# Moving the dense half and the coordinate products in TensorE's order of a fused attention and deformable-convolution kernel

## The reference, cut to what matters

```python
q, k, v = split(einsum('bchw,oc->bohw', group_norm(x), qkv_w) + qkv_b)   # 4 heads of 32
o = softmax(q @ k.T * hd**-0.5) @ v
feat_l = einsum(o, proj_w) + proj_b + x
...
offset_feat = conv1x1(concat([feat_l, feat_s * 2]), W_off)
om = conv3x3(offset_feat, W_om) + b_om            # 8 groups x 9 taps x (y, x, mask)
py, px = base + offset_y, base + offset_x         # per pixel, group and tap
val = bilinear(feat_s, py, px) * sigmoid(mask)    # four corners, zero outside
out = relu(einsum('bgckhw,ogck->bohw', val, W_dcn) + b_dcn) + feat_l
```

## Time and profile before

| what | value |
|---|---|
| median of 3 runs | 12684.2 us (12682.26 to 12689.32) |
| profiled execution, time | 12683.0 us |
| its span, first to last instruction | 12681.2 us |
| POOL busy | 10320.1 us (81%) |
| PE (TensorE matmul) busy | 9257.2 us (73%) |
| DVE (VectorE) busy | 7291.4 us (57%) |
| ACT (ScalarE) busy | 4747.5 us (37%) |
| POOL's indirect DMAs, L469 | 7168, mean 998 ns, with 949.5 us of issue between |
| POOL's additions, L465 | 13824, mean 250 ns |
| halves, L708, products | 12288, mean 356 ns |
| mean granted TensorE clock | 0.838 |

### The profile page before, as it was taken

The page is one execution under the profiler, slowest core; times in us unless marked ns, Lnnn a source line. Parts: engine busy times, 40 slices in busy tenths (PEclk is TensorE's granted clock), DMA queues, the critical chain, the costliest instruction groups (busy, mean ns, idle before and its releaser), DMA issues. The chain is left out here.

```text
span 12681.2 us, 168047 instructions
## 1 busy us (share of the span) xinstructions
PE 9257.2 (73%) x56052; PEld 5057.7 (40%) x56052; DVE 7291.4 (57%) x10291; ACT 4747.5 (37%) x6104; POOL 10320.1 (81%) x21509
## 2 busy tenths in 40 slices
PE   4677778775778777776577777777577777777754
PEld 1244444442444444443244344444234444444444
DVE  4356566644666666664566666665456666666443
ACT  1344444432434434433244344343233434334322
POOL 0278888885788888888488888888858888888888
PEclk7888888886888888888788888888788888888876
DMA  1222211110011111111011111111101111111100
GB/s 48 77 67 70 66 23 24 24 24 23 21 33 25 24 24 25 25 24 29 13 25 33 24 24 25 25 23 24 28 16 31 25 25 25 25 23 24 24 22 21
DMA packets 373774, 373.51 MB, mean 29 GB/s; under 512 B 129440, under 2 KB 219936, under 8 KB 372768
## 3 DMA queue, kind: packets, MB, share of 16 engines
q0 software_dynamic: 229376, 235.34, 8.9%
q10 hardware_dynamic: 97920, 71.35, 1.8%
q1 hardware_dynamic: 45472, 54.53, 1.6%
HBM read 316.66 MB, written 44.04 MB: 28 GB/s over the span
## 5 line engine op out<-in xcount | busy, mean ns | idle before, releaser
L469 POOL DMA_INDIRECT g<-patches,idx x7168 | 7156.6, 998 | 1112.4 <-issue 949.5
L905 DVE TENSOR_REDUCE mx<-ring 128x2 f32<-128x1024 f32 x2048 | 2411.1, 1220 | 2919.3 <-PE ring L666 2381.8
L541 ACT ACTIVATE p<-ring 128x1024 f32<-128x1024 f32 x2048 | 1984.8, 1021 | 3832.3 <-PE ring L724 2960.3
L465 POOL TENSOR_TENSOR carrier<-carrier 128x1 f32<-128x1 f32 x13824 | 3063.5, 250 | 122.0
L708 PE MATMUL ps_x<-fx,hats 128*128 128x208 f32 x12288 | 2520.1, 356 | 120.4 <-DVE hats L1048 78.8
L721 PE MATMUL ring<-qf,kf 32*128 32x512 f32 x8192 | 1459.9, 786 | 1515.3 <-ACT hats L551 816.3
L708 PEld LDWEIGHTS ps_x<-fx,hats 128*128 128x128 f32 x12288 | 2192.2, 196 | 671.2 <-issue 598.1
L734 PE MATMUL ps_a<-p,v 128*64 128x512 f32 x4096 | 1442.3, 790 | 39.0 <-DVE shared L932 37.6
L734 PE MATMUL ps_b<-p,v 128*64 128x512 f32 x4096 | 1247.2, 692 | 0.0
L1067 DVE TENSOR_TENSOR ps_x<-ps_x,chosen 128x416 f32<-128x416 f32 x1024 | 611.1, 597 | 1053.2 <-PE ps_x L708 844.1
L574 ACT COPY vt<-ps_x 128x256 f32<-128x256 f32 (+1 forms) x512 | 204.5, 399 | 2659.1 <-PE ps_x L780 1505.9
(11 more groups left out here) (125 smaller groups left out, 7601.4 us busy)
## 6 DMA issues: line engine op xcount, KB each, us to landing
g<-patches,idx POOLq DMA_INDIRECT x7168
patch_in<-in_fpad ACTq DMA_DIRECT2D x544, 64.0 KB
patches<-patch_out ACTq DMA_DIRECT2D x136, 256.0 KB
fx<-in_fpad SPq DMA_DIRECT2D x20, 416.0 KB
p<-in_x SPq DMA_DIRECT2D x4, 2048.0 KB
xq<-in_x SPq DMA_DIRECT2D x32, 256.0 KB
fs_s<-in_fs SPq DMA_DIRECT2D x32, 256.0 KB
xs<-in_x SPq DMA_DIRECT2D x32, 256.0 KB
```

The source lines that it names most:

```text
L465: last = nc.gpsimd.tensor_tensor(carrier[:, col:col + 1], carrier[:, 0:1], carrier[:, 0:1], ALU.add)
L469: nc.gpsimd.indirect_dma_start(out=g[:, j, :], out_offset=None, in_=patches[b], in_offset=bass.IndirectOffsetOnAxis(ap=idx[:, t, j:j + 1], ...
L541: nc.scalar.activation(p[:, (2 * kt + pair) % 4, :, :], ring[slot][:, :, :], ACT.Exp, scale=SCALE)\
L905: V.tensor_reduce(mx[:, n:n + 2, c], ring[slot][:, :, :], AX.X, ALU.max).then_inc(ring_free[slot], 1)
```

## The change

On TensorE a dense half moves from behind the maximum products to between scores and weigh, and `distances` from behind the turned part to right behind the first maximum's products (not in key tile 0). On VectorE `dense_half` moves ahead of `maxima` (and of `new_features`). On ScalarE `cut_hats` moves from behind the next key tile's exponentials to right behind `distances_to_hats`. Every key tile has at most one half, so `halves[1:]` is empty, and the slots of the turned taps come out as before. The ring's order, the semaphores and POOL's and SyncE's programs stay.

```diff
# constants: the turned taps get explicit slots; with two dense taps they are the old ones
-LAST_TAPS = CUTS[PARTS] - CUTS[PARTS - 1] + DENSE
+DENSE_CUTS = (0, 0, 0, 0, DENSE)
+WIDTHS = tuple(CUTS[part + 1] - CUTS[part] + DENSE_CUTS[part + 1] - DENSE_CUTS[part] for part in range(PARTS))
+SLOTS = tuple(sum(WIDTHS[:part]) for part in range(PARTS))
+HATS = 2
# ScalarE, step
                         exps(s, uses, kt + 1)
...
-                    for r, t, i in weighed_at(s, kt):
-                        cut_hats(uses, t, i)
...
                     for r, t, i in hats_at(s, kt):
                         distances_to_hats(uses, t, i)
+                        cut_hats(uses, t, i)
# TensorE, step
-                    maxima = maxima_at(s, last, kt)
+                    maxima, halves = maxima_at(s, last, kt), halves_at(s, kt)
                     if attends(s):
                         if 1 <= kt < KT - 1:
                             scores(s, uses, kt + 1)
...
+                    for r, t, i, half in halves[:1]:
+                        blocks_of_half(b, r, t, i, half, second)
+                    if attends(s):
                         weigh(s, uses, kt)
...
                         scores_for_max(uses, ("max", m), m)
                     if kt == 0 and projects(s - 1):
                         project(s - 1, uses)
-                    for r, t, i, half in halves_at(s, kt):
+                    if kt > 0:
+                        for r, t, i in hats_at(s, kt):
+                            distances(uses, r, t, i)
+                    for r, t, i, half in halves[1:]:
                         blocks_of_half(b, r, t, i, half, second)
                     for r, t in aligned_at(s, kt):
                         align(tile_number(r, t))
...
                     if kt == 0 and projects(s - 1):
                         offset_features(s - 1, uses)
-                    for r, t, i in hats_at(s, kt):
-                        distances(uses, r, t, i)
+                    if kt == 0:
+                        for r, t, i in hats_at(s, kt):
+                            distances(uses, r, t, i)
# VectorE, step
+                    halves = halves_at(s, kt)
+                    for r, t, j, half in halves[:1]:
+                        dense_half(r, t, j, half)
                     if kt == 0 and projects(s - 1):
                         new_features(s - 1, uses)
                     for m in maxima_at(s, last, kt)[:1]:
                         maxima(uses, ("max", m), m)
-                    for r, t, j, half in halves_at(s, kt):
+                    for r, t, j, half in halves[1:]:
                         dense_half(r, t, j, half)
```

More of the change, by code:

```diff
@@ L41 @@
 CUTS = tuple(min(2 * part, PICKED - (PARTS - part)) for part in range(PARTS + 1))
-LAST_TAPS = CUTS[PARTS] - CUTS[PARTS - 1] + DENSE
+DENSE_CUTS = (0, 0, 0, 0, DENSE)
+WIDTHS = tuple(CUTS[part + 1] - CUTS[part] + DENSE_CUTS[part + 1] - DENSE_CUTS[part] for part in range(PARTS))
+SLOTS = tuple(sum(WIDTHS[:part]) for part in range(PARTS))
+SLOT_TAPS = tuple(tap for part in range(PARTS) for tap in (*range(CUTS[part], CUTS[part + 1]),
+                                                           *range(PICKED + DENSE_CUTS[part], PICKED + DENSE_CUTS[part + 1])))
+HATS = 2
 KT_TILE = KT // SUB
@@ L136, in build @@
         dpos = sb("dpos", [128, SUB, 3, UNITS])
-        hats = sb("hats", [128, 2, 1 + PAIRS, SET_GROUPS * 128])
+        hats = sb("hats", [128, HATS, 1 + PAIRS, SET_GROUPS * 128])
         chosen = sb("chosen", [128, UNITS, BLOCKS])
@@ L238, in halves_at @@
         def halves_at(s, kt):
-            return tuple((r, t, i, half) for half in range(2) for r, t, i in sets_with(s, kt, half))
+            return tuple((r, t, i, half) for half in (1, 0) for r, t, i in sets_with(s, kt, half))
         def sampled_at(s, kt):
@@ L325, in build @@
         assert all(slots_in(o) % 2 == 0 for o in (FIRST, MID, LAST))
-        assert MID[-1][0] == "rows" and MID[0][0] == ("scores", 0)
+        assert ("rows", 2) in MID and MID[0] == (("scores", 0), 2)
         BATCH_SLOTS = USES_KV + slots_in(FIRST) + (STEPS_B - 2) * slots_in(MID) + slots_in(LAST)
@@ L556, in cut_hats @@
                 uses.wait_read(act, ("hats", t, i))
-                made = hats[:, i % 2, :, :]
+                made = hats[:, i % HATS, :, :]
                 for half in range(2):
@@ L571, in keep_turned @@
                 m = part_number(r, t, part)
[L572 removed]
+                width = WIDTHS[part] * 128
                 act.wait_ge(val_turned, m + 1)
[L574 removed]
+                nc.scalar.copy(vt[:, SLOTS[part]:SLOTS[part] + WIDTHS[part], :].rearrange("p k n -> p (k n)"), turned[:, 0:width]).then_inc(vt_ready, 1)
             def step(s, b, i):
@@ L707, in blocks_of_half @@
                     for pair in range(PAIRS):
-                        last = mm(cells, hats[:, i % 2, 1 + pair, j * 128:(j + 1) * 128], fx[:, pair, :, group * GC:(group + 1) * GC],
+                        last = mm(cells, hats[:, i % HATS, 1 + pair, j * 128:(j + 1) * 128], fx[:, pair, :, group * GC:(group + 1) * GC],
                                   start=pair == 0, stop=pair == PAIRS - 1)
@@ L766, in align @@
                 pe.wait_ge(vt_ready, n * PARTS + PARTS)
-                for tap in range(TAPS):
-                    last = mm(aligned, wdcn_s[:, tap, :], vt[:, tap, :], start=tap == 0, stop=tap == TAPS - 1)
+                for k, tap in enumerate(SLOT_TAPS):
+                    last = mm(aligned, wdcn_s[:, tap, :], vt[:, k, :], start=k == 0, stop=k == TAPS - 1)
                 last.then_inc(vt_used, 1)
@@ L780, in turn_part @@
                     last = tr(turned[:, i * 128:(i + 1) * 128], val[:, i * 128:(i + 1) * 128], ident_s[:, :])
-                if part == PARTS - 1:
-                    for d in range(DENSE):
-                        last = tr(turned[:, (picked + d) * 128:(picked + d + 1) * 128], dval[:, t % 2, d * C:(d + 1) * C],
-                                  ident_s[:, :])
+                for k, d in enumerate(range(DENSE_CUTS[part], DENSE_CUTS[part + 1]), picked):
+                    last = tr(turned[:, k * 128:(k + 1) * 128], dval[:, t % 2, d * C:(d + 1) * C], ident_s[:, :])
                 last.then_inc(val_turned, 1)
```

6 lines of the change are left out of this document (2 added, 4 removed).

## The result

The changed kernel takes 14086.4 us (14082.6 to 14090.4, 3 runs) against 12684.2: ratio 1.1105, 95% interval 1.1079 to 1.1130. It is slower by 1402 us. The forecast was 13950, in 12900 to 15000; it is 136 us short.

The account below looks back on a forecast made before the run. POOL's 361 us a step was taken to bound the kernel, over 345 for the other engines. Adding 56 us of waiting and 6 of clock makes their step 407; steps, image starts and end sum to 13950 us, range 12900 to 15000.

Parts of the forecast that it names:

- attention side's own step: TensorE, VectorE and ScalarE, chained through the ring, alone need 345 us per step of four POOL tiles.
- mark at the first image start: POOL's start of tile 0 at the first image start, forecast at 3514 us, 3215.7 before.
- The bound and the slack: POOL paces most steps at 361 us; the other engines need 345, leaving 16 us of slack a step.
- The odd key tile: Scores behind maximum products lose the half as cover and wait 2.47 us: +2.0 us in each of 14 key tiles.
- The even key tile: Distances wait 1.3 us for one slot, and the half now stands ahead: +2.0 us in each of 14 key tiles.
- The new wait for the hats' product: In even key tiles, half 0 waits for VectorE's hats' product: 0.4 us taken, bounds nothing to 1.9.
- The clock: More waiting lowers TensorE's granted clock from 0.88 to 0.86, adding 6 us a step.
- The whole: The other engines instead of POOL set the time; 407 us steps, image starts and end sum to 13950 us.
- No change: Rival: the moved half costs under 0.5 us a key tile, POOL's pace stays, 12684 us; chance 0.04.
- faster: Rival: the wait for ScalarE behind the distances goes and the half finds cover, 12590 us; chance 0.08.
- Milder: Rival: costs hold but the clock stays up or even key tiles gain; step 368, 12920 us; chance 0.13.
- Collapse: Rival: TensorE's clock falls to 0.70, step 471, 15650 us; chance of worse than 14690 us 0.12.

Follow-up runs that it names:

- e7: The kernel before with one instead of two tiny POOL additions ahead of each gather: 12133.8 us, ratio 0.9556.
- e3: The kernel before with the half moved in odd key tiles only, on TensorE and VectorE; coordinates and hats as before: 13313.2 us, ratio 1.0502.
- e11: e3 plus six products that nobody reads behind the maximum products of odd key tiles: 13125.1 us, ratio 1.0358.
- e6: The changed kernel with one instead of two tiny POOL additions ahead of each gather: 13905.2 us, ratio 1.0949.
- e2: The kernel before with only distances moved right behind the maximum products and hats cut early; halves in the old place: 13352.2 us, ratio 1.0536.
- e12: The changed kernel plus unread products: six behind odd key tiles' maximum products, five behind even ones' turned part: 13641.7 us, ratio 1.0733.
- e4: The changed kernel with VectorE back in its old order, maxima before the half: 14967.6 us, ratio 1.1802.
- e8: e2 with ScalarE making the distances to hats ahead of the copy of the turned part: 12783.6 us, ratio 1.0070.
- e9: The kernel before with even key tiles' half split around the distances and ScalarE's distances to hats ahead of the turned copy: 12709.4 us, ratio 1.0008.
- e10: e9 with one instead of two tiny POOL additions ahead of each gather: 16205.4 us, ratio 1.2778.

## Why the prediction was right, and where it was not

| step of the prediction | forecast us | measured us | shown by |
|---|---|---|---|
| attention side's own step | 345 | 344.4 | e7 |
| waiting of the odd key tiles, a step | 28 | 18.2 | waits in a step (21.7 - 3.5) |
| waiting of the even ones | 28 | 27.1 | waits in a step (15.2 + 3.9 + 8.0) |
| clock, a step | +6 | +23.6 | windows; e3, e11 |
| step after | 407 | 413.0 | POOL's marks |
| start of an image | 530 | 534 | POOL's marks |
| mark at the first image start | 3514 | 3478 | POOL's marks |
| images 2 and 3, each | 3379 | 3434, 3437 | POOL's marks |
| last image, to its last mark | 2849 | 2903 | 13252.06 - 10349.31 |
| end | 827.4 | 832.4 | 14084.5 - 13252.1 |

**The bound and the slack.** Right, and shown by taking the other side's load away: e7 gives the attention side's 344.4, e6 keeps after's 413.0.

**The odd key tile.** The wait behind the maximum products came as written, 2.46 us. But it comes 10 times a step and not 14. In 3 of the 14 odd key tiles the alignment products (`align`, 2.27 us) stand ahead of the scores and cover it; there the scores wait 0.35 us. In a fourth, key tile 3, the convolution's products (L765) stand there and wait 1.3 us for the maxima, and the scores behind them 0.7. I had counted the key tiles by the maxima they hold and not read what else stands between. TensorE's timeline of after, one of the three:

```profile
4794.74 1.14 PE L725 MATMUL ring<-qf,kf 32*128 32x512 f32 x8 [0.35 <-DVE mx L914]
```

**The even key tile.** The sum is right (27.1 against 28): the distances wait 1.33 us for one slot, the wait for ScalarE is 0.3 longer. The new wait for the hats' product is right in size (8.0 us a step against 14 x 0.4 = 5.6) and wrong in place. It is nothing in most key tiles, where the scores run at the lower clock for a part or in whole (1.3 to 2.09 us), the lower end of my own bounds; it is some 0.2 us in the three key tiles behind alignment products, where they run at the upper one (1.14 us), and 7.35 us in key tile 0. That the moved half costs nothing in key tiles 0 to 2 and 31 is wrong with it: I had looked at the maximum products alone and not at VectorE's projection.

**The clock.** This is the step that was mis-sized: +6 forecast, +23.6 measured. I took 0.86 between the 0.88 of the whole step and the 0.50 of the image start, and divided the same work by it. The row says 0.84, and e7 shows that the starting point is 0.90: the 0.88 of the earlier trace rows was read where POOL already held TensorE up for a part (idle 74 us in 348, in e7 69 in 344). The waits come right ahead of the products that last longest: the halves are busy 103.3 us a step instead of 76.0, 27.3 more, and all others together 3.7 less. The Trainium skill's rule (TensorE: Matmul & The Clock Gate, "Part 1: The HAM clock gate"), weighed in the prediction, pointed the right way for the whole change, 0.90 to 0.84. As the prediction put it, that more waiting means more time at 1.2 GHz, it does not hold in e2: 33 us more waiting a step, and 0.90 as in e7. e11 and e12, where idle products bring time back, show that the clock is a cause of its own and not only a companion of the waiting.

So a waiting 10.6 us too large and a clock term 17.6 too small nearly cancel. That the step came out within 6 us is in part luck.

**The whole.** The first steps of image 1 are cheaper than forecast: the first mark moved by 16 us and not by 33, and the next two steps grew by 44 us each (745.3 to 833.5 for both), not by 62. What already lengthened them before seems to cover a part; no run tests this. An image has one step of 430 us, the second. That is no cost of the change; in e7 this step takes 358 against 344 around it. I had missed it because before, POOL's pace covered it. The sum is -36 at the first image start, +55 and +58 for images 2 and 3, +54 and +5: +136.

**The rivals.** No change and faster are out: POOL waits 31 times. Milder would have needed a clock that rises; it fell to 0.84. Collapse did not come, although e4 shows the way to it: 0.80 in a step, 445 us. What the faster case wanted, cover between distances and next scores, works in e8; there the distances wait for VectorE in place of it, and POOL's pace and the start of image 1 hide whether anything is gained.

## What to carry to other kernels

On a two-slot ring whose users wait for both slots, the work that stands directly behind the producer of a slot is cover; moving it to where nothing waits costs the consumer's whole latency, here 2.3 us each time, ten times a step. Price such a move by listing every instruction between the producer and the next user in each kind of tile, on both engines. If the engine is TensorE, add what the clock may take from the products behind the waits. Here that is half as much again as the waiting itself, but it goes with the place: waits of the same size ahead of the distances (e2) cost none. And when one engine paces another, unload the pacer first to see what the other side's step is (one line here, and at 12133.8 us the best version).

## What the hardware showed that was not expected

- Waits of 2.46 us in ten more key tiles of a step, with the half moved behind the scores that follow them, took the granted clock of a step from 0.90 to 0.84, and a half from 2.38 us to 3.2 in the mean (up to 4.35). Six idle products behind the maximum products of 14 key tiles brought 10 us a step back (e11).
- Waits of 2.3 us in the mean, 14 a step, ahead of the distances left the clock at 0.90 (e2).
- Two edits that are harmless by themselves (e7 12133.8, e9 12709.4) give 16205.4 us together (e10), with 4101.7 us of ScalarE's and 3055.6 of VectorE's waiting for a releaser that the trace calls remote. The cause is open.
- POOL's pace for the same program of POOL was 89.68 us a tile in e8 and 90.87 in e9, on the same chip, with only the order of other engines changed.
